# Sharing the state product between VectorE and GpSimd, and moving the cell gathers, in a one-core hybrid kernel

## The chip, the cores and the metric

The kernel runs on one core of a Trainium2 chip. The metric is device time of one execution, in microseconds, as the median of several runs. The core's engines are TensorE (PE; its weight loads are PEld), VectorE (DVE), ScalarE (ACT), GpSimd (POOL) and SyncE (SP), which here only issues transfers. L872 means line 872 of the kernel before.

## The reference, cut to what matters

A tensor x of 16 images x 32 channels x 16 x 16 pixels passes four layers, each added to the stream with a norm:

- L0: an attention over pixels with pooled keys.
- L1: a Mamba block. For 64 inner channels and 16 states it runs `h = exp(dt * A) * h + dt * u * B[t]` and `y = sum over n of h[n] * C[n]` over time, for every image.
- L2: a windowed attention with 8 heads, then a mixture of 8 experts, two of which are chosen for each token.
- L3: attention in blocks of 32 nodes. Its mask and weights come from 1,048,576 edges (row, column, value): an edge inside one block sets the mask of its cell to 1 and writes its value there; the last edge of a cell wins. Only rows and columns below 256 matter. Then a small feed-forward part whose steps are picked at run time.

The output is the stream after that, of the shape of x.

## The kernel before

Activations lie as 128 partitions (4 images x 32 channels) by 1,024 columns (4 groups of 256 pixels). Each engine has one instruction stream in a hand-written order; semaphores tie them together.

**Edges.** The edge list (8 MB) comes in four chunks of 2 MB (`load_edges`, L637) on SyncE's queue, between the small weight loads: chunk 0, W_p and w_o, chunk 1, the 37 loads of `load_w1`, chunks 2 and 3. ScalarE turns the integers of a chunk to floats (`edge_floats`, L952), GpSimd subtracts columns from scaled rows (`edge_keys`, L733), VectorE picks the 8 largest keys of every 256 (`edges`, L1215). Then VectorE sorts out 48 slots for each partition and computes their fields (L1334). For 16 slots at a time (`CHUNK`), `hot_rows` (L1360) makes one-hot rows on VectorE, `weigh_planes` (L618) makes weighed one-hot columns on GpSimd, and TensorE adds their products in PSUM (`put_chunk`, L1924). The planes that result are copied by ScalarE (L1076), turned by TensorE (L1938), and VectorE reads them off as a table that holds, for each of 8,192 cells, the number of its edge or none (`planes_to_table`, L1374; `table_indices`, L1368; semaphore `tab_dve`). GpSimd gathers the 64 columns of values with 64 indirect transfers of 128 elements (`gather`, L858), multiplies them with the mask (L931), stores both in DRAM (L935) and loads them in the form of the blocks (L940; semaphore `bias_in`). VectorE builds bias, mask and gates from them in `bias_and_gates` (L1572), called in the expert loop before its fifth step. If a partition had more edges than slots, a slow path would run; with this input it does not.

**The scan of L1.** 64 steps, i = 16 j + n, for the four groups j of 1,024 columns and the 16 states n (a partition holds a channel of one of two states' halves). For step i: SyncE loads B in broadcast form (two transfers of 256 KB, L673; four buffers, two of them in dA, which was also the buffer of one-hot rows); GpSimd multiplies it with dt * u to dBu (L872, two buffers), then issues gather i - 1; ScalarE computes exp(dt * A) into PSUM (L1090, two buffers); VectorE runs the recurrence of a whole step in one scan instruction (L1432, three buffers `h_buf`); TensorE spreads C over the partitions into banks 2 and 3 (L1997, one buffer); VectorE multiplies state and C to hC (L1450, two buffers); TensorE adds hC to the sum in banks 6 and 7 (L2013). VectorE's order is scan(i + 1), product(i). After the last product of a group VectorE gates it (`gate_group`, L1435). dt is a softplus; its last two steps (L854, L856) are done by VectorE for j = 0 and by GpSimd, before the scan, for j = 1 to 3.

**Behind the scan.** Output projection, norm, then GpSimd clears two buffers (L882 to L884), the window attention runs on all four compute engines (GpSimd in L908, L919, L921), then GpSimd goes on with the mask product and the bias transfers (L931 to L940), and with a buffer that keys need later (L947). The expert loop (L1624), norm(5) (L1638), and the block attention of L3 follow.

## Time and profile before

| | us |
|---|---|
| median of 3 runs | 687.41 (687.07 to 688.64) |
| profiled execution | 686.04 |
| its span | 684.4 |
| busy: TensorE | 442.3 (65%) |
| busy: VectorE | 492.1 (72%) |
| busy: ScalarE | 200.8 (29%) |
| busy: GpSimd | 347.5 (51%) |

The page gives busy times, the span in 40 slices, the chain of work that ended last, and the costliest groups of instructions. In the slices VectorE and GpSimd are both at nine tenths or more from the 9th or 10th slice to the 21st, which is the scan. In the chain, GpSimd has 28% of the span, VectorE 24%, TensorE 21% and issue 16%; the two largest lines are L872 (12%) and L859 (8%). TensorE's granted clock was 0.824 of 2.4 GHz on the mean. A line of the order of time holds start, duration, engine, line, operation, output and inputs with their shapes, the count, and in brackets how long the engine had idled and what released it; a merged line covers several instructions.

### The profile page before, as it was taken

Reading aid. Unit: us, or ns where it says so; the run is one execution under the profiler, and the core shown is the slowest. Engines: PE = TensorE matmul, PEld = TensorE weight load, DVE = VectorE, ACT = ScalarE, POOL = GpSimd, SP = SyncE. Lnnn points to the kernel's source line nnn. Section 1 sums busy time; section 2 is a strip of 40 time slices with the busy share of each in tenths; the row PEclk is TensorE's granted clock in tenths of the full one; section 3 lists DMA queues with packets and bytes.
Section 4 is the critical chain, followed back from the end, with each engine's and each line's share of the span. In section 5 each row is a group of like instructions: output and inputs, shape, how many; then the busy total and the mean of one; then the engine's idle time right before and its main releaser. Section 6 shows DMA issues by size and latency. Waiting matters only on the chain.

```text
span 684.4 us, 8165 instructions
## 1 busy us (share of the span) xinstructions
PE 442.3 (65%) x2986; PEld 225.9 (33%) x2986; DVE 492.1 (72%) x627; ACT 200.8 (29%) x218; POOL 347.5 (51%) x285
## 2 busy tenths in 40 slices
PE   7644864147767668667667887985579964525560
PEld 2531313113223223222223344654355633523220
DVE  2946995789999999999995348877135548996332
ACT  2463692033333332333330543121020043012110
POOL 6626307969999999999992003657840000000000
PEclk9866885559999999999999999555569997678766
DMA  8340020545555554454530000000000000000000
GB/s 281 63 196 0 10 66 13 123 120 143 154 147 148 154 151 151 145 151 144 150 93 1 11 1 1 2 1 2 9 13 0 1 0 1 1 1 0 8 5 31
DMA packets 29252, 46.04 MB, mean 67 GB/s; under 512 B 17878, under 2 KB 19320, under 8 KB 28184
## 3 DMA queue, kind: packets, MB, share of 16 engines
q1 hardware_dynamic: 26776, 45.10, 22.8%
q0 software_dynamic: 2368, 0.37, 0.4%
q8 instruction: 25, 0.41, 0.2%
q14 instruction: 19, 0.16, 0.1%
q10 hardware_dynamic: 64, 0.00, 0.0%
HBM read 43.55 MB, written 1.11 MB: 65 GB/s over the span
## 4 chain that ended last, share of the span: by engine, by line
POOL 28%; DVE 24%; PE 21%; issue 16%; SPq 4%; ACT 4%; DMA 2%; DVEq 0%; POOLq 0%; ACTq 0%
POOL dBu L872 12%; POOL hit L859 8%; SPq L651 3%; PE ps L1875 2%; PE ps L2184 2%; POOL work L921 2%; POOL work L919 2%; PE ps L2085 2%; POOL work L908 2%; PE ps L2195 2%; DMA work<-in_L_attn_edge_index 1%; POOL hst L621 1%; PE ps L2341 1%; PE ps L1929 1%; PE ps L2013 1%
## 5 line engine op out<-in xcount | busy, mean ns | idle before, releaser
L2013 PE MATMUL ps<-hC,ident 128*128 128x512 f32 x256 | 121.7, 597 | 0.0
L1090 ACT ACTIVATE ps<-work,a_neg 128x1020 f32<-128x1020 f32 x64 | 71.3, 1115 | 164.5 <-DVE hst L1432 99.1
L1432 DVE TENSOR_TENSOR_SCAN hst<-ps,dBu 128x1024 f32<-128x1024 f32 x43 | 98.2, 2285 | 3.9 <-issue 1.3
L1997 PE MATMUL ps<-late,pick_state 96*128 96x512 bf16 x128 | 39.5, 391 | 84.3 <-DVE hC L1450 65.2
L872 POOL TENSOR_TENSOR dBu<-work,dA 128x1024 f32<-128x1024 f32 x32 | 75.5, 2361 | 2.8 <-DVE hst L1432 2.2
L872 POOL TENSOR_TENSOR dBu<-work,b_sb 128x1024 f32<-128x1024 f32 x32 | 75.9, 2373 | 0.6
L859 POOL DMA_INDIRECT hit<-in_L_attn_edge_values,tab_i x64 | 63.4, 990 | 12.8 <-issue 10.0
L2013 PEld LDWEIGHTS ps<-hC,ident 128*128 128x128 f32 x256 | 49.3, 193 | 43.6 <-issue 34.6
L1997 PEld LDWEIGHTS ps<-late,pick_state 96*128 96x128 bf16 x128 | 7.8, 97 | 135.1 <-DVE hC L1450 112.6
L1450 DVE TENSOR_TENSOR hC<-hst,ps 128x1024 f32<-128x1024 f32 x43 | 51.4, 1195 | 1.2 <-PE ps L1997 1.2
L1432 DVE TENSOR_TENSOR_SCAN work<-ps,dBu 128x1024 f32<-128x1024 f32 x21 | 48.0, 2285 | 1.4
L1810 PE MATMUL ps<-idle_bf,zero_bf 128*128 128x512 bf16 x122 | 37.7, 450 | 16.8 <-issue 13.4
L908 POOL TENSOR_TENSOR work<-work,sm 128x1024 f32<-128x1024 f32 x8 | 15.3, 1911 | 55.0 <-DVE sm L1537 55.0
L1000 ACT ACTIVATE sq<-ps 128x512 f32<-128x512 f32 x12 | 7.2, 597 | 85.7 <-PE ps L1875 68.4
L1522 DVE COPY_PREDICATED work<-band,ps 128x1024 f32<-128x1024 int32 x8 | 10.4, 1305 | 24.4 <-ACT work L1115 24.4
L621 POOL TENSOR_TENSOR hst<-hC,b_sb 128x2048 bf16<-128x2048 bf16 x3 | 11.8, 3934 | 30.6 <-DVE dBu L1364 27.1
L1450 DVE TENSOR_TENSOR hC<-work,ps 128x1024 f32<-128x1024 f32 x21 | 25.1, 1195 | 1.5 <-PE ps L1997 1.5
L1810 PEld LDWEIGHTS ps<-idle_bf,zero_bf 128*128 128x128 bf16 x122 | 12.1, 109 | 40.7 <-issue 29.7
L2138 PE MATMUL ps<-work 128*32 128x64 f32 (+1 forms) x512 | 14.6, 306 | 14.1 <-POOL work L921 14.1
L2114 PEld LDWEIGHTS ps<-work 32*128 32x128 f32 x512 | 21.5, 256 | 5.0 <-issue 5.0
L2114 PE MATMUL ps<-work 32*128 32x64 f32 x512 | 22.8, 346 | 0.0
L2126 PE MATMUL ps<-work,w_vu 32*128 32x256 f32 x64 | 15.9, 584 | 8.4 <-DVE work L1551 8.4
(358 smaller groups left out, 857.9 us busy)
## 6 DMA issues: line engine op xcount, KB each, us to landing
b_sb<-b_rows_all SPq DMA_DIRECT2D x64, 256.0 KB
dA<-b_rows_all SPq DMA_DIRECT2D x64, 256.0 KB
work<-in_L_attn_edge_index SPq DMA_DIRECT2D x6, 1024.0 KB, 6.3
dA<-in_L_attn_edge_index SPq DMA_DIRECT2D x1, 1024.0 KB, 10.5
dBu<-in_L_attn_edge_index SPq DMA_DIRECT2D x1, 1024.0 KB, 12.5
hit<-in_L_attn_edge_values,tab_i POOLq DMA_INDIRECT x64
late<-work SPq DMA_DIRECT2D x12, 64.0 KB, 2.0
X<-in_x SPq DMA_DIRECT2D x1, 512.0 KB, 3.9
```

Of the source, the lines that this page charges most:

```text
L621: return eng.tensor_tensor(plane_hot[k], col_hot[:, r, :].unsqueeze(2).to_broadcast([P, CHUNK, PLANES, C]), weighed[:, r, :].unsqueeze(3). ...
L651: sp.dma_start(dst, src).then_inc(dma_w1, 16)
L859: nc.gpsimd.indirect_dma_start(out=hit[:, i // C, 0, i % C:i % C + 1], out_offset=None, in_=a["L3_attn_edge_values"].rearrange("(e o) -> e ...
L872: nc.gpsimd.tensor_tensor(dBu[:, i % 2, :], dtu[:, j * NT:(j + 1) * NT], b_buf[i % 4], ALU.mult).then_inc(dbu_done, 1)
L908: nc.gpsimd.tensor_tensor(pairs(s2_buf[u % 3]), pairs(s2_buf[u % 3]), sm2[:, u % 2, :].unsqueeze(2).to_broadcast([P, SEGS, C]), ALU.mult). ...
L1090: nc.scalar.activation(dst[:, :, 1:], src[:, :, 1:], ACT.Exp, scale=a_neg[:, n:n + 1]).then_inc(dA_sb, 1)
L1432: V.tensor_tensor_scan(h_buf[i % 3], dA_ps[k], dBu[:, k, :], 0.0, ALU.mult, ALU.add).then_inc(scan_done, 1)
L1450: V.tensor_tensor(hC[:, k, :], h_buf[i % 3], bank(2, 2), ALU.mult).then_inc(hc_done, 1)
L1810: T.matmul(bank(k), zero_bf[:, :], idle_bf[:, :], start=True, stop=True, skip_group_check=True)
L1997: last = T.matmul(bank(2 + h), pick_state[:, n, :, :].rearrange("p v i -> p (v i)"), parts[:, j * NT + h * HALF:j * NT + (h + 1) * HALF], ...
L2013: last = T.matmul(bank(6 + h), ident[:, :], hC[:, i % 2, h * HALF:(h + 1) * HALF], start=False, stop=(n == S - 1))
L2114: last = T.matmul(bank(g)[:, 2 * C * m:2 * C * m + 2 * C], qm[r, j * WT + m, 4 * hg:4 * hg + 4, :].rearrange("p h q -> p (h q)"), xpad[r, ...
```

## The change

- The product of state and C (hC) is split by columns: VectorE takes the first 848 of 1,024 (704 in the last group), GpSimd the others. GpSimd can't read PSUM, so ScalarE copies these columns of the spread C into `c_sb` first; VectorE, too, waits for that copy. TensorE's second half of the sum waits for GpSimd's part.
- No gathers in the scan. 5 stand behind the table, 15 behind the clearing of the expert buffers, 44 behind the window attention. GpSimd's order in the scan is dBu(i + 2), share(i).
- GpSimd's part of dt for groups 1 to 3 moves into the scan, in pieces of 256 columns, one in every third state up to the tenth of the group before.
- `weigh_planes` is done by VectorE, in front of each block of one-hot rows; TensorE waits for one semaphore less.
- The planes are turned as before; ScalarE copies the turned planes to SBUF, the scan starts after that, and VectorE reads the table from the copy behind the last scan product, ahead of the last gating.
- `bias_and_gates` moves from the expert loop to the place between the expert output and norm(5).
- SyncE: the loads of L1 are fewer (24 for 37, some of them over more partitions with a repeated source); chunk 2 of the edges is issued after the 11th; the loads of B for step 0 are issued at once, for step 1 after the third block of one-hot rows, from step 2 on after the planes.
- ScalarE converts chunk 2 behind the copies of the turned attention and chunk 3 behind the first norm's root. GpSimd's key subtraction of chunk 2 moves ahead of the weight taps. TensorE's idle matmuls after L0 are 18 for 10.

```diff
@@ -139,6 +139,9 @@
         b_rows = area(0, 1)
+        DVE_COLS = (848, 848, 848, 704)
+        c_sb = [area(4, 1)[:, k * 320:(k + 1) * 320] for k in range(3)]
+        EARLY = 20
         b_dram = nc.dram_tensor("b_rows_all", [J, 2 * S, NT], F32, kind="Internal").ap()
@@ -235,9 +238,9 @@
         planes = area(22, 1).rearrange("p (g r) -> p g r", g=G)
...
-        inv_i = hC[:, 1, 0:G * 2 * C].rearrange("p (g c) -> p g c", g=G).bitcast(I32)
-        symbols = hC[:, 1, G * 2 * C:G * 2 * C * PLANES].rearrange("p (g k c) -> p g k c", g=G, c=2 * C)
+        turned = area(0, 1).rearrange("p (g r) -> p g r", g=G)
+        table_at = area(1, 1)
@@ -499,12 +504,13 @@
         def load_w1():
+            over = lambda n, v: bass.AP(v.tensor, v.offset, [[0, n]] + [list(x) for x in v.ap])
+            split = lambda n, t: t
             col = lambda v: v.rearrange("(c o) -> c o", o=1)
+            for dst, name in ((ln_g, "gamma"), (ln_b, "beta"), (b_p[:, :], "b_p")):
+                yield split(G, dst), over(G, col(a["L1_conv_" + name]))
             for g in range(G):
                 r = slice(C * g, C * g + C)
-                yield ln_g[r], col(a["L1_conv_gamma"])
-                yield ln_b[r], col(a["L1_conv_beta"])
-                yield b_p[r, :], col(a["L1_conv_b_p"])
                 yield win_nat[r, :, :], a["L1_conv_W_in"].rearrange("(r e) c -> e r c", e=C)
@@ -512,12 +518,11 @@
             yield s2[:, :], broadcast_rows(a["L1_conv_s2"], P)
+            for dst, name in ((conv_b, "conv_b"), (b_dt, "b_dt"), (d_skip, "D_skip")):
+                yield split(2, dst[:, :]), over(2, col(a["L1_conv_" + name]))
+            yield split(2, a_log[:, :]), over(2, a["L1_conv_A_log"])
             for v in range(2):
                 r = slice(64 * v, 64 * v + 64)
-                yield conv_b[r, :], col(a["L1_conv_conv_b"])
-                yield b_dt[r, :], col(a["L1_conv_b_dt"])
-                yield d_skip[r, :], col(a["L1_conv_D_skip"])
-                yield a_log[r, :], a["L1_conv_A_log"]
                 yield wx_t[r, :], a["L1_conv_W_x"].rearrange("n d -> d n")
@@ -647,9 +652,10 @@
             with nc.allow_non_contiguous_dma("small transposed weights"):
-                for dst, src in load_w1():
+                for k, (dst, src) in enumerate(load_w1()):
                     sp.dma_start(dst, src).then_inc(dma_w1, 16)
-            load_edges(2)
+                    if k == 10:
+                        load_edges(2)
             load_edges(3)
@@ -663,10 +669,13 @@
             sp.wait_ge(b_out, 16)
-            sp.wait_ge(planes_ps, 1)
             late_weights = load_w3()
...
                 j, n = i // S, i % S
+                if i == 1:
+                    sp.wait_ge(rows_sb, 3)
+                if i == 2:
+                    sp.wait_ge(planes_ps, 1)
                 if i >= 4:
@@ -801,6 +810,7 @@
                                   .to_broadcast([BC, S, 2, 64])).then_inc(w_rows_sb, 1)
+            edge_keys(2)
             pool.wait_ge(w1_dve, 1)
@@ -842,19 +851,6 @@
-            for q in range(SLOTS // CHUNK):
-                pool.wait_ge(rows_sb, max(2, q + 1))
-                if q >= 2:
-                    pool.wait_ge(hot_used, q - 1)
-                weigh_planes(nc.gpsimd, q % 2, q).then_inc(hot_sb, 1)
...
-            for j in range(1, J):
-                r = slice(j * NT, (j + 1) * NT)
-                pool.wait_ge(dt_log, j + 1)
-                nc.gpsimd.tensor_tensor(dt_act[:, r], dt_act[:, r], dtu[:, r], ALU.add).then_inc(dt_later, 1)
-                pool.wait_ge(dt_later, j)
-                link(nc.gpsimd.tensor_tensor(dtu[:, r], dt_act[:, r], u_act[:, r], ALU.mult))
...
             def gather(i, done=gathered):
@@ -862,32 +858,61 @@
-            for i in range(J * S):
+            def state_input(i):
...
                 j, n = i // S, i % S
...
                     pool.wait_ge(dtu_sb, 1)
+                    pool.wait_ge(hot_used, 2)
                 pool.wait_ge(b_in[i % 4], 32 * (i // 4 + 1))
...
                                         ALU.mult).then_inc(dbu_done, 1)
-                if i == 1:
-                    pool.wait_ge(tab_dve, 1)
-                if i >= 1:
-                    gather(i - 1)
-            gather(J * S - 1)
...
+            def state_share(i):
...
+                pool.wait_ge(scan_done, i + 1)
+                pool.wait_ge(c_copied, i + 1)
+                if i >= 2:
+                    pool.wait_ge(y_ps, i - 1)
+                cols = DVE_COLS[i // S]
+                nc.gpsimd.tensor_tensor(hC[:, i % 2, cols:], h_buf[i % 3][:, cols:], c_sb[i % 3][:, 0:NT - cols],
+                                        ALU.mult).then_inc(hc_pool, 1)
...
+            def later_delta(j, quarter):
...
+                r = slice(j * NT + quarter * N, j * NT + (quarter + 1) * N)
+                pool.wait_ge(dt_log, j + 1)
+                nc.gpsimd.tensor_tensor(dt_act[:, r], dt_act[:, r], dtu[:, r], ALU.add).then_inc(dt_later, 1)
+                pool.wait_ge(dt_later, 4 * (j - 1) + quarter + 1)
+                link(nc.gpsimd.tensor_tensor(dtu[:, r], dt_act[:, r], u_act[:, r], ALU.mult))
...
+            state_input(0)
+            state_input(1)
+            for i in range(J * S):
+                if i + 2 < J * S:
+                    state_input(i + 2)
+                state_share(i)
+                j, n = i // S, i % S
+                if j + 1 < J and n % 3 == 0 and n < 12:
+                    later_delta(j + 1, n // 3)
             assert J * S == 2 * C
...
+            pool.wait_ge(tab_dve, 1)
+            nc.gpsimd.memset(xpad[:, :, 0:C], 0.0).then_inc(filled, 1)
+            for i in range(EARLY // 4):
+                gather(i)
             pool.wait_ge(x_new, 2 * 2)
-            nc.gpsimd.memset(xpad[:, :, 0:C], 0.0).then_inc(filled, 1)
             nc.gpsimd.memset(eb_bd, 0.0)
             nc.gpsimd.memset(e_bd, 0.0).then_inc(filled, 1)
+            for i in range(EARLY // 4, EARLY):
+                gather(i)
...
             with pool.If(more > 0):
-                pool.wait_ge(gathered, 16 * 2 * C)
+                pool.wait_ge(gathered, 16 * EARLY)
                 with pool.Fori(0, EDGES // (P * GW)) as t:
@@ -927,6 +952,8 @@
             window_bands(UNITS - 1)
+            for i in range(EARLY, 2 * C):
+                gather(i)
             pool.wait_ge(gathered, 16 * 2 * C)
@@ -976,11 +1003,10 @@
                 nc.scalar.activation(pixels(att, h), pixels(att, h), ACT.Exp).then_inc(first_sb, 1)
-            edge_floats(2)
             for h in range(2):
...
                 nc.scalar.activation(pixels(att_t, h), bank(2 * h, 2), ACT.Copy).then_inc(first_sb, 1)
-            edge_floats(3)
+            edge_floats(2)
@@ -1006,6 +1032,7 @@
             inverse_root(rs4[:, :], bn2[:, :, 1], eps5).then_inc(rs4_sb, 1)
+            edge_floats(3)
@@ -1074,6 +1101,19 @@
             nc.scalar.activation(planes, ps[:, 0:4, 0:N], ACT.Copy).then_inc(planes_sb, 1)
+            act.wait_ge(b_out, 16)
+            act.wait_ge(planes_t, 1)
+            act.wait_ge(over_sb, 1)
+            nc.scalar.activation(turned, ps[:, 0:4, 0:N], ACT.Copy).then_inc(turned_sb, 1)
...
+            def state_out(i):
...
+                act.wait_ge(c_ps, i + 1)
+                if i >= 3:
+                    act.wait_ge(hc_pool, i - 2)
+                cols = DVE_COLS[i // S]
+                nc.scalar.activation(c_sb[i % 3][:, 0:NT - cols], bank(2, 2)[:, cols:],
+                                     ACT.Copy).then_inc(c_copied, 1)
@@ -1084,11 +1124,14 @@
                 elif n == 0:
-                    act.wait_ge(dt_later, j)
+                    act.wait_ge(dt_later, 4 * j)
                 src = dt_act[:, j * NT:(j + 1) * NT].rearrange("p (b t) -> p b t", t=N)
...
                                      scale=a_neg[:, n:n + 1]).then_inc(dA_sb, 1)
+                if i >= 1:
+                    state_out(i - 1)
+            state_out(J * S - 1)
             norm_steps(2, eps5)
@@ -1371,10 +1414,12 @@
-            def planes_to_table(dst, base, link):
...
-                weights = ps[:, 0:4, 0:2 * C]
-                shares = ps[:, 0:4, 2 * C:2 * C * PLANES].rearrange("p g (k c) -> p g k c", c=2 * C)
+            def planes_to_table(dst, base, link, source, room):
...
+                weights = source[:, :, 0:2 * C]
+                shares = source[:, :, 2 * C:2 * C * PLANES].rearrange("p g (k c) -> p g k c", c=2 * C)
+                inv_i = room[:, 0:G * 2 * C].rearrange("p (g c) -> p g c", g=G).bitcast(I32)
+                symbols = room[:, G * 2 * C:G * 2 * C * PLANES].rearrange("p (g k c) -> p g k c", g=G, c=2 * C)
                 k3_ = PLANES - 1
@@ -1403,11 +1448,11 @@
             dve.wait_ge(cols_sb, 1)
-            for q in range(2):
-                hot_rows(q, q).then_inc(rows_sb, 1)
...
-            dve.wait_ge(hot_used, 1)
-            hot_rows(0, 2).then_inc(rows_sb, 1)
+            for q in range(SLOTS // CHUNK):
+                if q >= 2:
+                    dve.wait_ge(hot_used, q - 1)
+                weigh_planes(V, q % 2, q)
+                hot_rows(q % 2, q).then_inc(rows_sb, 1)
             dve.wait_ge(dt_log, 1)
@@ -1415,11 +1460,9 @@
             V.tensor_copy(over_i[:, :], bank(0)[0:1, HALF - 1:HALF]).then_inc(over_sb, 1)
-            link(planes_to_table(tab[:, :], g_base[:, 0, :], link))
-            table_indices(link).then_inc(tab_dve, 1)
...
             dve.wait_ge(part_round, PARTS)
             dve.wait_ge(b_rows_sb, 1)
+            dve.wait_ge(turned_sb, 1)
             V.memset(dA_ps[0][:, 0:NT:N], 0.0)
@@ -1429,6 +1472,7 @@
                     dve.wait_ge(hc_done, i - 2)
+                    dve.wait_ge(hc_pool, i - 2)
                 V.tensor_tensor_scan(h_buf[i % 3], dA_ps[k], dBu[:, k, :], 0.0, ALU.mult,
@@ -1444,12 +1488,17 @@
                 dve.wait_ge(scan_done, i + 1)
-                dve.wait_ge(c_ps, i + 1)
+                dve.wait_ge(c_copied, i + 1)
                 if i >= 2:
                     dve.wait_ge(y_ps, i - 1)
-                V.tensor_tensor(hC[:, k, :], h_buf[i % 3], bank(2, 2), ALU.mult).then_inc(hc_done, 1)
+                cols = DVE_COLS[j]
+                V.tensor_tensor(hC[:, k, 0:cols], h_buf[i % 3][:, 0:cols], bank(2, 2)[:, 0:cols],
+                                ALU.mult).then_inc(hc_done, 1)
                 if n == 0 and j > 0:
                     gate_group(j - 1)
+            dve.wait_ge(turned_sb, 1)
+            link(planes_to_table(tab[:, :], g_base[:, 0, :], link, turned, table_at))
+            table_indices(link).then_inc(tab_dve, 1)
             gate_group(J - 1)
@@ -1622,8 +1671,6 @@
             for t in range(TT):
-                if t == 4:
-                    bias_and_gates()
                 dve.wait_ge(ex_ps, t + 1)
@@ -1635,6 +1682,7 @@
+            bias_and_gates()
             norm(5)
@@ -1868,7 +1916,7 @@
                     last.then_inc(first_ps, 1)
-            keep_warm(10, 7)
+            keep_warm(18, 7)
@@ -1978,7 +2026,6 @@
                 pe.wait_ge(rows_sb, q + 1)
-                pe.wait_ge(hot_sb, q + 1)
                 ends = q == SLOTS // CHUNK - 1
@@ -1992,7 +2039,7 @@
                     pe.wait_ge(c_in, 16 * PARTS * J)
-                    pe.wait_ge(tab_dve, 1)
+                    pe.wait_ge(turned_sb, 1)
                 for h in range(2):
@@ -2010,6 +2057,8 @@
                 for h in range(2):
+                    if h == 1:
+                        pe.wait_ge(hc_pool, i + 1)
                     last = T.matmul(bank(6 + h), ident[:, :], hC[:, i % 2, h * HALF:(h + 1) * HALF],
```

## Rows read from the trace of the kernel before

**Rows 1.** Order of time in the scan, GpSimd and VectorE: start, us, engine, line.

```profile
247.18 2.36 POOL L872 TENSOR_TENSOR dBu<-work,dA 128x1024 f32<-128x1024 f32 x1
...
249.57 2.29 DVE L1432 TENSOR_TENSOR_SCAN hst<-ps,dBu 128x1024 f32<-128x1024 f32 x1
```

**Rows 2.** Order of time, GpSimd at the end of the scan.

```profile
362.62 0.99 POOL L859 DMA_INDIRECT hit<-in_L_attn_edge_values,tab_i  x1 [0.16 <-issue]
363.91 0.94 POOL L859 DMA_INDIRECT hit<-in_L_attn_edge_values,tab_i  x1 [0.30 <-issue]
```

**Rows 3.** Order of time, two of VectorE's products early in the scan.

```profile
158.47 1.20 DVE L1450 TENSOR_TENSOR hC<-hst,ps 128x1024 f32<-128x1024 f32 x1
...
161.78 1.19 DVE L1450 TENSOR_TENSOR hC<-hst,ps 128x1024 f32<-128x1024 f32 x1
```

**Rows 4.** Order of time from 30 to 68 us.

```profile
30.32 0.85 SPq L640 DMA_DIRECT2D work<-in_L_attn_edge_index  x2
...
39.25 1.91 ACT L955 ACTIVATE work<-work 128x2048 f32<-128x2048 int32 x1 [10.57 <-DMA work<-in_L_attn_edge_index]
...
47.67 0.75 DVE L1274 SCALAR_TENSOR_TENSOR X<-ps,gamma,X 128x512 f32<-128x512 f32 x1 [8.45 <-PE ps L1865]
...
62.93 1.41 DVE L1222 MAX8 hC<-work 128x8 f32<-128x256 f32 x4 [3.24 <-POOL work L738]
...
66.67 1.87 DVE L1310 TENSOR_SCALAR x<-xn,w_in 128x512 f32<-128x512 f32 x1
```

**Rows 5.** Order of time from 94 to 145 us.

```profile
94.73 1.76 DVE L1356 TENSOR_TENSOR hC<-rows_at,b_sb 128x1536 bf16<-128x1536 bf16 x1
...
96.52 3.23 DVE L1364 TENSOR_SCALAR dA<-rows_at,b_sb 128x256 bf16<-128x256 bf16 x16
...
118.38 3.60 PE L1929 MATMUL ps<-dA,hst 32*128 32x256 bf16 x64 [5.28 <-POOL hst L621]
...
124.31 0.40 DVE L1379 TENSOR_SCALAR hC<-ps 128x256 int32<-128x256 int32 x1
...
142.49 4.47 DVE L1432 TENSOR_TENSOR_SCAN hst<-ps,dBu 128x1024 f32<-128x1024 f32 x2 [1.25 <-issue]
```

**Rows 6.** Order of time in the scan: TensorE's broadcast of C, ScalarE's exponential.

```profile
249.50 0.60 PE L1997 MATMUL ps<-late,pick_state 96*128 96x512 bf16 x2 [1.20 <-DVE hC L1450]
...
251.90 1.12 ACT L1090 ACTIVATE ps<-work,a_neg 128x1020 f32<-128x1020 f32 x1 [2.41 <-DVE hst L1432]
```

**Rows 7.** Groups of GpSimd's instructions by line and form: count, busy us, mean ns.

```profile
L921 POOL TENSOR_TENSOR work<-work,band 128x896 f32<-128x896 f32 x8 | 16.6, 2076 | 0.0
...
L806 POOL TENSOR_TENSOR work<-w_in,work 128x256 f32<-128x256 f32 x2 | 1.7, 851 | 18.4 <-DVE w_dt L1305 18.4
...
L769 POOL TENSOR_TENSOR centerer<-ident,averager 128x128 f32<-128x128 f32 x1 | 0.5, 455 | 0.1
```

**Rows 8.** Order of time, VectorE's last gating behind the scan.

```profile
373.46 1.22 DVE L1438 TENSOR_TENSOR work<-work,ps 128x1024 f32<-128x1024 f32 x1 [5.59 <-PE ps L2013]
```

**Rows 9.** Order of time from 489 to 557 us: GpSimd, then VectorE, then TensorE.

```profile
489.96 0.31 POOL L931 TENSOR_TENSOR hit<-hit 128x64 f32<-128x64 f32 x1
...
493.73 4.64 POOL L940 DMA_DIRECT2D late<-cell_bias  x8 [1.59 <-DMA cell_bias<-hit]
...
529.12 0.07 DVE L1576 MEMSET late<- 128x8 f32 x1
...
536.16 1.22 DVE L1631 TENSOR_TENSOR work<-ps,work 128x1024 f32<-128x1024 f32 x1 [0.44 <-PE ps L2195]
...
554.40 0.69 DVE L1293 TENSOR_TENSOR xn<-ps,rstd 128x512 f32<-128x512 f32 x1 [3.93 <-ACT rstd L995]
...
556.39 3.70 PE L1815 MATMUL ps<-xn,nat 128*128 128x512 f32 x8 [1.25 <-DVE xn L1293]
```

**Rows 10.** Order of time, GpSimd's first instruction of the window attention.

```profile
414.72 1.91 POOL L908 TENSOR_TENSOR work<-work,sm 128x1024 f32<-128x1024 f32 x1 [29.81 <-DVE sm L1537]
```

**Rows 11.** Busy times in stretches: length, each engine's busy us, granted clock, DMA.

```profile
565.00:570.00 5.00, 2.64 (x11) 1.17 (x12) 4.51 (x5) 2.03 (x2) 0.00 (x0) 0.61 0.00 0
```

9 lines of the change are left out of this document (5 added, 4 removed).

## The prediction

> **What bounds the kernel now.** I read the page first (busy shares, the 40 slices, the chain that ended last), then the order of time in four stretches: 30 to 70 us, 92 to 145 us, some steps of the scan, and 486 to 570 us. The scan is a third of the span and VectorE is nearly always busy there, yet it isn't the bound. GpSimd multiplies dBu in 2.36 us [rows 1], idles 0.16 us, issues a gather in 0.99 us [rows 2] and goes straight on to the next product: 3.53 us, all of it GpSimd's own work. VectorE's scan (249.57) starts just as that product ends (247.18 + 2.36 = 249.54). Where GpSimd is not late, VectorE's products follow each other after 3.31 us [rows 3]. So the scan runs at GpSimd's pace, and the chain of waits passes through dBu and the gathers, hardly through the product hC.
>
> **Part 1, the first 80 us.** [rows 4] ScalarE waits 10.57 us for chunk 2 of the edges, converts it, and only then copies the turned attention, for which TensorE and then VectorE (8.45 us of idle time) wait. The chunk was issued at 30.32, after 37 small loads, and landed by 39.25. In the change it is issued after 11 of 24 loads (about 15 us) and converted behind the copies, so its landing, 8.9 us after issue by this row and some more behind chunk 1, no longer decides; VectorE is free at 47.67 - 8.45 = 39.2, and the attention's output can be there by then. Chunk 3 is converted behind the first norm's root, near 43 us; issued near 25 us it has landed. GpSimd subtracts the keys 13 to 18 us earlier, so VectorE's wait for them (3.24) goes, and with it the lengthening of the affine step beside one: 1.87 us for 512 columns, where a product of 1,024 columns takes 1.19 [rows 3], so about 0.6 would do, 1.3 less. Sum: 8.45 + 3.24 + 1.3 = 13.0 us. From there VectorE has an unbroken queue to the slot columns, so all of it arrives. Bounds: 8.5 (keys still late, or the 8 added warm-up matmuls outlast the weights at the low clock) to 14.
>
> **Part 2, the planes.** [rows 5] From the first block of compares (96.52) to the first scan (142.49) it is 46.0 us: weighing on GpSimd, a third block behind it, the table read while GpSimd multiplies. Now VectorE weighs before each block. That isn't in the trace; a product of 1,536 bf16 columns took 1.76, so 2,048 take 2.3, and a block of compares 3.2: 3 x 5.5 = 16.5. Then TensorE's last chunk 3.6; planes copied, turned and the overflow flag read, 2.3 (from 121.98 to 124.31); ScalarE's new copy of the turned planes 1.0 (estimate: 1,024 columns, as the exponential's 1.12 [rows 6]); hand-overs 0.5; and 1.3 from the cleared columns to the first scan, as now (141.23 to 142.49). That is 25.2, a gain of 20.8 us. Bounds 17 (weighing at twice the row) to 22. SyncE's loads of B for states 1 and 2 wait for block 3 and the planes, with the rest of B queued behind; the first state's no longer does. A product dBu after them has about 2 us to spare before its scan, so this hides.
>
> **Part 3, the scan.** The gather leaves GpSimd's step; a share of hC comes in, 176 of 1,024 columns, 320 in the last quarter. The same operation takes 0.455 us at 128 columns and 2.076 at 896, which gives 0.55 and 0.86, less 0.03 of overlap; the 256-column row of 0.851 (other strides) is the upper end [rows 7]. I take the line, since the share is contiguous as its two ends are. GpSimd's step: 2.32 + 0.52 = 2.84, in the last quarter 3.15. In the first three quarters GpSimd also computes the next delta in four pieces of two 256-column products, 2 x 0.72 + 0.15 = 1.6 each. A quarter is 16 x 2.84 + 6.4 = 51.8, three times, then 50.4: 205.8. VectorE alone: 3.31 less 0.18 (0.33 in the last quarter), 3.13 and 2.98, with three gatings 201. GpSimd stays the bound, by little. Before, it is 225.4 from the first scan's start to the last product's end (367.87, 5.59 before the gating of [rows 8]). With 1 us for start and end the gain is 18.5 us; bounds 4 (share and pieces at 0.851) to 24 (VectorE's pace). The new waits: GpSimd's share waits for ScalarE's copy, and behind it in GpSimd's queue stands the product dBu of three states on. The copy comes after the product (0.93), TensorE's broadcast (0.60) and itself, 0.3 to 0.5: 2.0 us after a scan's end, while dBu ends at 2.3 [rows 6]. Hidden, with 0.3 us to spare. TensorE's second half of the sum waits for the share, which precedes VectorE's part: hidden.
>
> **Part 4, the table behind the scan.** 13 operations of the bias step, most on 256 columns, take 5.4 us (529.12 to 536.16 - 0.44 - 1.22) [rows 9]; the table's 15 have about 1,000 columns more: 6.2. They lie in the 5.59 us in which VectorE waits for TensorE before the last gating [rows 8]. Cost 0.6; with that cover gone, 6.2. Five gathers then run beside the norm, where VectorE has two SBUF-to-SBUF affine steps; no gather stands beside one in the trace. Between 0 and 2 x 0.99 [rows 2]: 0.5.
> The Trainium skill (SBUF — State Buffer, Who interferes with whom) says that GpSimd and a VectorE operation in a two-port mode, or one with two SBUF inputs against a GpSimd read, block each other for a whole instruction. The trace agrees for products (the 1.87 above); for gathers no run here shows it. By it this term would be up to 2.0.
>
> **Part 5, the late gathers.** All 64 lay under the scan's pace; now 5 come behind it, 15 behind its output (20 us in 29.8 us of idle time [rows 10]) and 44 after the window attention. Two gathers without a product between them start 1.29 us apart [rows 2]. From 490.0: 44 x 1.29 = 56.8, the last one out by 546.6, landed by 548.3 (1.6, as the 1.59 that GpSimd waited for its own store). From the mask product (489.96) to the bias in SBUF: issues to 498.37 and a landing of 1.6, 10.0 us [rows 9]. The bias lands at 558.2. VectorE, free at 550.5, builds it until 563.6 and norms in 1.3: 564.9 against 556.3, 8.6 us lost. In the experts' loop the removed step gives nothing: the next product but one waited for TensorE anyway (0.44). TensorE now idles 10 us before eight matmuls that took 3.70; after the next idle stretch, of 6 us, its granted clock was 0.61 [rows 11], halfway down to 1.2 GHz, and at that level they take 7.4: I add 3.0. Sum 11.6 lost.
> The Trainium skill (DMA: Bandwidth & Descriptors, Latency and other measured facts) gives about 1 us for GpSimd's emission of a software DMA. The trace agrees with the busy part (0.99) and shows 0.30 us of idle time on top. By the page alone, an estimate, 44 take 44 us and this is rival (a).
>
> **Sum.** -13.0 - 20.8 - 18.5 + 0.6 + 0.5 + 11.6 = -39.6 us. The profiled execution took 686.04 us (span 684.4), 1.4 below the median of the runs: 646.4, and 647.8 as a median. Measurement here tells 0.2% (1.4 us) from no change.
>
> **Rivals.** (a) The gathers go out at their busy time, 1.0 us: the bias lands at 546, in time; the moved step then costs what it exceeds VectorE's wait for the root (5.4 against 3.93 [rows 9]), 1.5, and no clock is lost: 637.7. Against it stands the one pair. It decides at 1.1 us apart. (b) The share and the pieces are dear, 0.85: the scan gains 4 only, 662. (c) On SyncE's one queue the small loads stand behind the 2 MB of chunk 2 and hold the first norms; part 1 gives 5: 656. Against: 13 loads are out 15 us before they are read. (d) Gathers hold up the router's 17 short VectorE operations, most with two SBUF inputs, each by up to one gather of 0.99, some 10 us in all: 658; this is the skill's lock, told above, with the trace silent. (e) Slower: ScalarE's copy stands behind an exponential, 1.12 us [rows 6]. It is ready 3.1 us after a scan's end, GpSimd waits 0.8 in each step, and a step costs 3.65, with the delta pieces 4.05: the scan takes 33 us more than before, against 21.1 gained elsewhere: 699. It decides from 3.88 us a step. Against: in ScalarE's order the copy of state i precedes the exponential of i + 2. (f) The edits do not take effect on the path at all: 687; each moves work off a stretch that waits, so 1 in 100.
>
> **Chances.** Forecast 0.52 (its own bounds 640 to 655), (a) 0.17, (b) 0.12, (c) 0.08, (d) 0.07, (e) 0.03, (f) 0.01. The range takes in (a), (c), (d) and most of (b): 635 to 660. Faster 0.96, same 0.01, slower 0.03.
>
> **What the profile after would show.** Part 1: the attention's residual on VectorE near 39 us. Part 2: the first scan near 108. Part 3: dBu products 2.84 apart where no delta piece stands between, 3.15 at the end, GpSimd hardly idle; if it waits for the scan instead, VectorE is the bound. Part 4: the last gating at most 1 us behind TensorE. Part 5: 1.29 between gathers, VectorE waiting for the bias, a lower clock in the four projections. Wrong altogether if a scan step exceeds 3.5 us.

## The result, and the profile after

The changed kernel takes 701.25 us (median of 4 runs, 701.0 to 702.52) where before takes 687.89 (4 runs, 687.07 to 688.64): the ratio is 1.0199, with a 95% interval of 1.0183 to 1.0215. So it takes 2.0% longer, clear of no change, though the interval reaches to both sides of 2%; and it is 53 us above the forecast. The span of the profiled execution is 699.5 us. Of all runs named here one, of the kernel before beside the fifth experiment (1,408.53 us), was a slow one and is left out.

The page of after, busy times and slices (each slice is 17.5 us):

```profile
PE 449.7 (64%) x2994; PEld 229.3 (33%) x2994; DVE 470.2 (67%) x630; ACT 217.6 (31%) x283; POOL 369.9 (53%) x364
DVE  3989987999999999996126878200052468976421
POOL 6574017999999999993531765977760000000000
PEclk9888877999999999999979555556559986768775
```

The scan ends in slice 19 (317 us), three slices earlier than before. But slices 27 to 29 are nearly empty for DVE (0 0 0, from 455 to 507 us), exactly where GpSimd shows 7, 7 and 7: the late gathers. To see where that gap begins, both orders of time are cut at the same operations:

| stretch | before | after | difference |
|---|---|---|---|
| start to the first scan | 142.49 | 108.10 | -34.4 |
| scans, to the last product's end | 225.4 | 209.0 | -16.4 |
| table, gating, projection, norm | 11.3 | 12.5 | +1.3 |
| norm to the window attention's input | 8.4 | 11.2 | +2.8 |
| from there to the first unit's weights on GpSimd | 27.2 | 36.1 | +8.9 |
| window units, to the last band product | 75.3 | 75.2 | 0 |
| to VectorE's residual X | 1.9 | 13.5 | +11.6 |
| to the copy of the router's results | 16.9 | 48.5 | +31.7 |
| experts, to their residual | 40.4 | 41.5 | +1.1 |
| to norm(5), with the moved bias step in after | 5.2 | 6.6 | +1.4 |
| block attention, to its residual | 68.3 | 69.4 | +1.1 |
| to the first pick of the last part | 8.7 | 8.7 | 0 |
| the steps picked at run time, to the end | 53.0 | 59.1 | +6.0 |

Up to the norm behind the scan the change gained 49.5 us, nearly the 51.2 that the forecast had to there. Then 55.0 us are lost in four stretches, in each of which, or just ahead of it, gathers go out back to back, and 6.0 in the last steps. These are the rows of after that answer to those shown of before. VectorE, in order of time, for [rows 4, 5]:

```profile
39.12 0.73 DVE L1317 SCALAR_TENSOR_TENSOR X<-ps,gamma,X 128x512 f32<-128x512 f32 x1
...
94.36 2.28 DVE L626 TENSOR_TENSOR hst<-hC,b_sb 128x2048 bf16<-128x2048 bf16 x1
96.56 3.22 DVE L1407 TENSOR_SCALAR dA<-rows_at,b_sb 128x256 bf16<-128x256 bf16 x16
...
105.29 0.15 DVE L1462 CAST over_i<-ps 1x1 int32<-1x1 f32 x1 [3.12 <-PE ps L1986]
...
108.10 2.29 DVE L1476 TENSOR_TENSOR_SCAN hst<-ps,dBu 128x1024 f32<-128x1024 f32 x1 [1.25 <-ACT ps L1130]
```

One step of the scan, for [rows 1, 3, 6, 7]:

```profile
252.69 0.55 POOL L880 TENSOR_TENSOR hC<-hst,work 128x176 f32<-128x176 f32 x1
252.77 2.29 DVE L1476 TENSOR_TENSOR_SCAN work<-ps,dBu 128x1024 f32<-128x1024 f32 x1 [0.60 <-POOL dBu L870]
252.86 0.32 ACT L1115 ACTIVATE work<-ps 128x176 f32<-128x176 f32 x1 [1.81 <-PE ps L2044]
253.07 1.11 ACT L1130 ACTIVATE ps<-work,a_neg 128x1020 f32<-128x1020 f32 x1
253.21 2.35 POOL L870 TENSOR_TENSOR dBu<-work,b_sb 128x1024 f32<-128x1024 f32 x1
254.97 1.01 DVE L1495 TENSOR_TENSOR hC<-hst,ps 128x848 f32<-128x848 f32 x1
```

The share takes 0.55 us as forecast, and ScalarE's copy stands ahead of the exponential and costs 0.32.

Now the stretch behind the window attention. VectorE and TensorE, for [rows 9]:

```profile
465.73 1.41 DVE L1616 SCALAR_TENSOR_TENSOR X<-ps,b_u,X 128x512 f32<-128x512 f32 x2 [20.91 <-remote]
...
514.26 0.42 DVE L1651 COPY work<-ps 128x256 f32<-128x256 f32 x1 [35.24 <-remote]
```

```profile
454.29 0.42 PE L2187 MATMUL ps<-work 128*32 128x64 f32 x6 [0.28 <-issue]
455.02 0.35 PE L2187 MATMUL ps<-work 128*32 128x32 f32 x5 [0.30 <-issue]
466.53 3.78 PE L1923 MATMUL ps<-X,centerer 128*128 128x512 f32 x4 [11.17 <-issue]
...
488.14 0.21 PE L2222 MATMUL ps<-rb_row,one_row 1*128 1x32 f32 x1 [0.82 <-issue]
490.24 0.21 PE L2223 MATMUL ps<-r_bd,xn 128*128 128x32 f32 x1 [1.90 <-issue]
493.04 0.21 PE L2223 MATMUL ps<-r_bd,xn 128*128 128x32 f32 x1 [2.59 <-issue]
```

In before the same two instructions of VectorE, residual and copy, stand 16.9 us apart, and their waits are put down to TensorE:

```profile
491.95 1.41 DVE L1567 SCALAR_TENSOR_TENSOR X<-ps,b_u,X 128x512 f32<-128x512 f32 x2 [9.35 <-PE ps L2138]
...
508.81 0.42 DVE L1602 COPY work<-ps 128x256 f32<-128x256 f32 x1 [7.15 <-PE ps L2174]
```

In after, too, both of VectorE's waits are for TensorE: for the last window output, and for the last of 32 router matmuls. TensorE stands idle between matmuls that wait for no semaphore ("issue"), and its records lie a multiple of 0.70 us apart (488.14, 488.84 for a weight load, 490.24, 491.64, 493.04). The trace notes the semaphore of the last matmul (record 493.04) only at 514.24; so a record here does not tell when the work was done, and what is held up must be read from VectorE's side. The 128x512 matmuls of the norm take 3.78 us as in before: long ones are not slower. In the trace of before no matmul without a wait of its own is held like that.

Meanwhile GpSimd keeps its pace, as forecast from [rows 2]:

```profile
452.36 0.99 POOL L855 DMA_INDIRECT hit<-in_L_attn_edge_values,tab_i  x1 [0.15 <-issue]
453.65 0.94 POOL L855 DMA_INDIRECT hit<-in_L_attn_edge_values,tab_i  x1 [0.30 <-issue]
...
509.06 0.32 POOL L958 TENSOR_TENSOR hit<-hit 128x64 f32<-128x64 f32 x1 [2.02 <-DMA hit<-in_L_attn_edge_values,tab_i]
...
512.83 4.65 POOL L967 DMA_DIRECT2D late<-cell_bias  x8 [1.59 <-DMA cell_bias<-hit]
```

The bias lands near 519, 67 us behind the last band product (68.2 in the forecast). It is wanted at 557. The wait that the forecast had priced never happened, because all else was later.

### The profile page after: what moved, and what is told of

Read it like the earlier page. It is cut to its first block, busy times and chain, and to the rows that moved or that the text cites. A ratio compares the mean times of both kernels' runs of the same rounds, so it can differ in the third digit from the quotient of the medians.

```text
span 699.5 us, 8496 instructions
## 1 busy us (share of the span) xinstructions
PE 449.7 (64%) x2994; PEld 229.3 (33%) x2994; DVE 470.2 (67%) x630; ACT 217.6 (31%) x283; POOL 369.9 (53%) x364
## 4 chain that ended last, share of the span: by engine, by line
DVE 34%; PE 25%; issue 15%; ACT 10%; POOL 8%; another core or an unknown queue 5%; DVEq 1%; DMA 1%; ACTq 0%; POOLq 0%
DVE hC L1495 8%; ACT ps L1130 7%; PE ps L2044 5%; PE ps L2244 2%; PE ps L2134 2%; PE ps L2233 2%; POOL work L946 2%; PE ps L1923 2%; POOL dBu L870 2%; DVE hC L1269 2%; POOL work L944 2%; POOL work L933 2%; PE ps L1863 2%; DVE hC L1265 2%
## 5 line engine op out<-in xcount | busy, mean ns | idle before, releaser
L870 POOL TENSOR_TENSOR dBu<-work,b_sb 128x1024 f32<-128x1024 f32 x32 | 75.3, 2353 | 41.4 <-DVE work L1459 39.2
L855 POOL DMA_INDIRECT hit<-in_L_attn_edge_values,tab_i x64 | 60.8, 950 | 19.1 <-issue 19.1
L1115 ACT ACTIVATE work<-ps 128x176 f32<-128x176 f32 (+1 forms) x64 | 22.2, 347 | 121.4 <-PE ps L2044 121.4
L1858 PE MATMUL ps<-idle_bf,zero_bf 128*128 128x512 bf16 x130 | 40.0, 451 | 16.8 <-issue 14.6
L1495 DVE TENSOR_TENSOR hC<-hst,ps 128x848 f32<-128x848 f32 (+1 forms) x43 | 41.8, 973 | 1.2 <-ACT work L1115 1.2
L2244 PE MATMUL ps<-x,xn 128*128 128x512 f32 x32 | 18.0, 698 | 24.2 <-DVE work L1662 24.2
L880 POOL TENSOR_TENSOR hC<-hst,work 128x176 f32<-128x176 f32 (+1 forms) x43 | 27.4, 636 | 2.3 <-ACT work L1115 2.3
L2163 PE MATMUL ps<-work 32*128 32x64 f32 x512 | 25.6, 353 | 4.5 <-issue 4.5
L2163 PEld LDWEIGHTS ps<-work 32*128 32x128 f32 x512 | 23.5, 262 | 10.2 <-issue 10.2
```

The source lines that it names most:

```text
L855: nc.gpsimd.indirect_dma_start(out=hit[:, i // C, 0, i % C:i % C + 1], out_offset=None, in_=a["L3_attn_edge_values"].rearrange("(e o) -> e ...
L870: nc.gpsimd.tensor_tensor(dBu[:, i % 2, :], dtu[:, j * NT:(j + 1) * NT], b_buf[i % 4], ALU.mult).then_inc(dbu_done, 1)
L880: nc.gpsimd.tensor_tensor(hC[:, i % 2, cols:], h_buf[i % 3][:, cols:], c_sb[i % 3][:, 0:NT - cols], ALU.mult).then_inc(hc_pool, 1)
L1495: V.tensor_tensor(hC[:, k, 0:cols], h_buf[i % 3][:, 0:cols], bank(2, 2)[:, 0:cols], ALU.mult).then_inc(hc_done, 1)
L1858: T.matmul(bank(k), zero_bf[:, :], idle_bf[:, :], start=True, stop=True, skip_group_check=True)
L2163: last = T.matmul(bank(g)[:, 2 * C * m:2 * C * m + 2 * C], qm[r, j * WT + m, 4 * hg:4 * hg + 4, :].rearrange("p h q -> p (h q)"), xpad[r, ...
```

## The experiments

**Theory G:** gathers that go out back to back hold up the issue of instructions on TensorE, and so each stretch in which it issues many short ones. In the scan of before, where nothing of the kind is seen, they went out 3.53 us apart:

```profile
246.17 0.99 POOL L859 DMA_INDIRECT hit<-in_L_attn_edge_values,tab_i  x1 [0.16 <-issue]
...
249.70 0.99 POOL L859 DMA_INDIRECT hit<-in_L_attn_edge_values,tab_i  x1 [0.16 <-issue]
```

**Rivals:** B, any unbroken run of GpSimd does it; C, it is the moved bias step and TensorE's low clock, not the gathers; a price for each gather, wherever it stands; and S, the many reads of one address. For the last 6 us, **theory L:** the place of the loop's code in the instruction stream.

### The late gathers left out, replaced, drawn apart, made direct

The first and the fourth edit are shown against the kernel after, the second and the third against the first. The values that these kernels leave out or get wrong are read only behind the copy of the router's results.

```diff
-            for i in range(EARLY, 2 * C):
-                gather(i)
-            pool.wait_ge(gathered, 16 * 2 * C)
+            nc.gpsimd.memset(hit[:, 0, 0, EARLY:C], 0.0)
+            link(nc.gpsimd.memset(hit[:, 1, 0, :], 0.0))
+            pool.wait_ge(gathered, 16 * EARLY)
```

> The kernel after without its 44 late gathers (two memsets write their cells instead, so values are left out). Theory G (gathers that go out back to back hold up TensorE where it runs many small matmuls): the window attention still starts 11.7 us late behind the 15 gathers ahead of it, but from its last GpSimd product (452) the residual follows after 2 us, and the router's copy 17 us after the residual as before, not 48.5: COPY near 471, and 175.6 us from there to the end as before plus 1.5 for the moved bias step: 649 us. Rival C (TensorE's low clock or the moved bias step itself is what costs): the router's stretch stays near 48 us and the time near 695.

In the second kernel a memset stands for each gather:

```diff
+            for i in range(EARLY, 2 * C):
+                link(nc.gpsimd.memset(dBu[:, 0, :], 0.0))
```

> The kernel after with each of the 44 late gathers replaced by a GpSimd memset of 1,024 columns (0.94 us, as a gather's busy time; values left out). Theory G: the stall belongs to the gathers as transfers: no stall, 650 us. Rival B (any unbroken run of GpSimd instructions holds TensorE up): residual to router copy stays near 48 us, time near 700.

In the third, 14 gathers with fillers:

```diff
+            for i in range(EARLY, EARLY + 14):
+                gather(i)
+                link(nc.gpsimd.memset(dBu[:, :, :], 0.0))
+                link(nc.gpsimd.memset(dBu[:, 0, 0:512], 0.0))
```

> The kernel after with 14 of the 44 late gathers, each followed by two memsets so that they go out about 3.5 us apart as in the scan of before (30 left out). If the stall needs gathers close together (theory G with density): no instruction of TensorE stalls, residual to router copy 17 us, time 651. If each gather has its price whatever the distance (43 us / 44 = 1.0 each): 14 us more, 665.

In the fourth, all 44 as plain transfers:

```diff
-                gather(i)
+                nc.gpsimd.dma_start(hit[:, i // C, 0, i % C:i % C + 1],
+                                    a["L3_attn_edge_values"][P * i:P * i + P].rearrange("(p o) -> p o", o=1)
+                                    ).then_inc(gathered, 16)
```

> The kernel after with the 44 late gathers as plain GpSimd transfers of 128 x 4 bytes from the values (wrong values, indices left out). If software transfers of many small pieces are the cause, whatever computes their addresses: the same stall, time 690 to 705. If it is the gather's indirect form: no stall, 650 or less.

Measured, one run each, beside one of before of 689.75 us: 659.52, 659.61, 661.45 and 658.10 us. The kernel with 14 gathers 3.63 us apart, VectorE:

```profile
455.67 1.41 DVE L1620 SCALAR_TENSOR_TENSOR X<-ps,b_u,X 128x512 f32<-128x512 f32 x2 [9.65 <-PE ps L2191]
...
472.33 0.43 DVE L1655 COPY work<-ps 128x256 f32<-128x256 f32 x1 [7.81 <-PE ps L2227]
```

From residual to copy it is 16.7 us in all four (before 16.9, after 48.5), and VectorE's releaser is TensorE again. B falls: 44 memsets hold nothing up. C falls: the copy comes at 470.7 without late gathers, as expected near 471. A fixed price falls, at least at 3.63 us apart. And it is the gather's form, or something that comes with it, since plain transfers of 128 x 4 bytes went out 0.54 us apart (13 in 7.03 us), more than twice as densely, and held nothing up:

```profile
453.32 7.03 POOL L956 DMA_DIRECT2D hit<-in_L_attn_edge_values  x13
```

Nor is it the traffic that the transfers make. The software queue carried as many packets in the kernel after as in the one with plain transfers:

```profile
q0 software_dynamic: 2368, 0.37, 0.4%
```

```profile
q0 software_dynamic: 2368, 0.37, 0.5%
```

The times were 8 to 11 us above what was expected (649 to 651). I had carried the end of before over unchanged; in the first of these kernels the last steps take 60.5 us for 53.0, and the block attention 2.3 us more. So the last steps are a loss of their own.

### All gathers kept, but apart; the distance; the addresses

The fifth kernel puts a memset behind each gather outside the window attention, puts 24 gathers inside it, and the bias step behind norm(5):

```diff
+            def spaced(i):
+                gather(i)
+                link(nc.gpsimd.memset(dBu[:, 0, :], 0.0))
...
                 if u >= 1:
                     window_bands(u - 1)
+                for i in range(EARLY + 3 * u, EARLY + 3 * u + 3):
+                    gather(i)
```

> The kernel after with all 64 gathers kept but drawn apart: 20 ahead of the window attention and 20 behind it each followed by a memset (about 2.3 us apart), 24 inside it (three in a row behind each unit's band products); the bias step behind norm(5), in VectorE's 5.5 us wait for the projections. If gathers 2.3 us apart and three in a row hold nothing up: the 2.8 + 8.9 + 11.6 + 31.7 = 55 us of held-up stretches and 1.4 us of the bias step go: 701.25 - 56.4 = 645 us. If every gather has its price whatever the distance: 64 x 1.0 stay, 695 to 705. If three in a row already stall: 650 to 670.

The sixth, against the first:

```diff
+            for i in range(EARLY, EARLY + 22):
+                gather(i)
+                link(nc.gpsimd.memset(dBu[:, 0, :], 0.0))
```

> The kernel after with 22 of the 44 late gathers, one memset behind each, so about 2.3 us apart (22 left out). At 3.63 us apart nothing stalled (661.45 us, router's copy 16.7 us behind the residual). If the limit lies below 2.3 us: again 661. If the stall grows steadily with density: router's copy 25 us or more behind the residual, 670 to 680.

The seventh, against after:

```diff
-                    in_offset=bass.IndirectOffsetOnAxis(ap=tab_i[:, i:i + 1], axis=0)).then_inc(done, 16)
+                    in_offset=bass.IndirectOffsetOnAxis(ap=any_i[:, i:i + 1], axis=0)).then_inc(done, 16)
...
+            link(nc.gpsimd.iota(any_i[:, :], pattern=[[1, 2 * C]], base=0, channel_multiplier=8192))
```

> The kernel after with every gather reading 128 different addresses, spread over the whole list (values not the table's). In the table only 2,417 of 8,192 cells hold an edge, the others all read edge 0. Rival S (it is the many reads of one address, which the direct transfers did not have either): no stall, 650 to 660 us. If it is the gather's form and pace: unchanged, 48.5 us from residual to router copy, 701.

Spread, the kernel takes 661.33 us (two runs) against 687.57 and 689.69 for before, a ratio of 0.9603 (0.9518 to 0.9689): 40 us better than after, 4% better than before. Residual and copy stand where they should (2.1 us and 16.7), but 645 was missed by 16. GpSimd came to the first unit's weights at 372.33, 3.9 us after VectorE had its sums ready; the units took 83.4 us for 75.3, since three gathers with their gaps filled up to 4.5 us of a unit (384.21 to 388.69), more than the 4.2 us that GpSimd idles there in before, and GpSimd then worked without a break; the last steps took 59.6 us. The total lies in the range that was expected if three in a row already stall (650 to 670), and only the trace speaks for the other reading. The sixth kernel (one run), at 2.19 us apart, had 16.7 us from residual to copy, and took 662.25: no stall there. In the seventh (one run) all 64 gathers read different addresses, and it took 47.2 us from residual to copy (468.21 to 515.45), with the same records 1.40 us apart at the end of the router. S falls. Its total, 901.6 us, says nothing on this: with other values in the mask one of the last steps alone took 197 us, which I did not follow up.

### The code's place, first try

```diff
+            for _ in range(PAD):
+                dve.wait_ge(x_new, 1)
```

> The kernel after with 63 added wait instructions on VectorE, all already met, in its 19 us wait ahead of the first window unit; nothing else changed. VectorE's stream in after is 65 instructions longer than before ahead of the final steps, and in those steps it stands still 3.1 us behind two branches beside 8 KB instruction loads, which before does not show. Theory L (the code's place decides whether the loop's branches wait for code): 65 + 63 = 128 instructions of 64 bytes are one load, the steps return to their 53.0 us from the first pick to the end (59.1 in after): 695 us. If it is something else: 701.

It measured 717.72 us (one run), 16.5 more than after, and not what either theory expects; all of it lies between the norm behind the scan and the first unit's weights (63.7 us for 47.3). The kernel sets the name PAD itself further down, so 144 wait instructions came in, not 63, and the question of theory L was not put. But the run shows what the stall is better than any other. All 144 waits were already met; this is VectorE's own queue at that line, with least, median and longest duration in ns and first and last start:

```profile
L1565 DVEq EVENT_SEMAPHORE  x144: 1/50/709, 337.1 to 365.2; - x144
```

At its ordinary pace VectorE gets through such waits every 0.098 us, all 144 in 14 us; here they take 28. The 15 gathers ahead of the window attention go out from 337.7 to 356.1. From 340.9 to 359.0, about 3 us behind both, a record of these trivial waits lasts 0.70 us time and again, with a few short ones between (a selection, start and duration in us):

```text
340.824 0.050 Vector EVENT_SEMAPHORE
340.922 0.269 Vector EVENT_SEMAPHORE
342.649 0.706 Vector EVENT_SEMAPHORE
343.374 0.696 Vector EVENT_SEMAPHORE
...
357.544 0.695 Vector EVENT_SEMAPHORE
359.093 0.050 Vector EVENT_SEMAPHORE
359.191 0.050 Vector EVENT_SEMAPHORE
```

These instructions touch no SBUF and no PSUM, and VectorE is another engine than TensorE. So the instructions themselves are held back, on both engines, in pieces of 0.70 us: I call it their issue, though the records do not tell whether they are late in being issued or late in reaching the engine.

### Gathers placed by what TensorE issues, and the code's place again

Against the fifth kernel, with 18 gathers inside the window attention and 21 ahead of it:

```diff
-            for i in range(EARLY // 4, EARLY):
-                spaced(i)
+            for i in range(5, 15):
+                gather(i)
+            for i in range(15, EARLY):
+                spaced(i)
...
+                if u < INSIDE // 3:
+                    for i in range(EARLY + 3 * u, EARLY + 3 * u + 3):
+                        gather(i)
```

> As e5_spread, but the gathers placed by what TensorE issues: 5 drawn apart behind the scan, 10 back to back while TensorE runs only 512-column matmuls, 6 drawn apart ahead of the window units, three in a row behind each of the first six units and none behind the last two, 25 drawn apart behind the window attention. In e5_spread GpSimd came to the first unit's weights 3.9 us late and the units took 83.4 us for 75.3: 3.9 and some 6 of the 8.1 should go: 651 us. If the ten back to back hold TensorE up all the same: 660.

The tenth adds 63 instructions to VectorE, counted this time:

```diff
+            for k in range(FILL):
+                V.memset(pad[:, k:k + 1], 0.0)
             dve.wait_ge(o2_ps, UNITS)
```

> As e9_placed with 63 one-element memsets more on VectorE, in its 9.4 us wait for the window output (e8_pad had meant to add 63 and added 144). 65 + 63 = 128 instructions of 64 bytes make one 8 KB load, so the final loop stands to the loads as in before. Theory L (position of the loop's code): from the first pick to the end 53 us for 59, 6 us less than e9_placed: 645 us. If it is something else: no difference.

Measured: 655.68 us (ratio to before 0.954, 0.9524 to 0.9556) and 649.85 us (0.9453, 0.9437 to 0.9468), each 5 us above what was expected (651 and 645). In the ninth kernel the ten gathers back to back do hold TensorE up: VectorE's first masking of scores (356.25) comes 18.2 us behind the window attention's input, for 14.3 in before, while GpSimd stands idle for 8.9 us until it gets the first unit's weights. And the units took 78.9 us for 75.3.

The 63 useless instructions make the kernel 5.8 us faster. One of the last steps, VectorE, in the ninth and then the tenth kernel:

```profile
613.49 0.14 DVE L1772 CAST ctrl<-code 1x1 int32<-1x1 f32 x1
...
628.01 2.47 DVE L1837 TENSOR_SCALAR work<-ps,work 128x1024 f32<-128x1024 f32 x2 [11.73 <-PE ps L2391]
...
636.65 0.14 DVE L1772 CAST ctrl<-code 1x1 int32<-1x1 f32 x1
```

```profile
615.29 0.14 DVE L1776 CAST ctrl<-code 1x1 int32<-1x1 f32 x1
...
625.13 2.47 DVE L1841 TENSOR_SCALAR work<-ps,work 128x1024 f32<-128x1024 f32 x2 [7.04 <-PE ps L2395]
...
634.65 0.14 DVE L1776 CAST ctrl<-code 1x1 int32<-1x1 f32 x1
```

23.2 us from the second pick to the third fall to 19.4, and 39.6 from the second pick to the end to 33.2. The loads of 8 KB of instructions from the first pick to the end, in the queue table of that stretch, for the ninth and then the tenth:

```profile
q14 instruction: 11, 0.09, 0.5%
```

```profile
q14 instruction: 3, 0.02, 0.1%
```

Before has 4 of them, after 11. Theory L holds, and the other kernels bear it out. With 754, 755 or 881 instructions on VectorE ahead of the first pick (before, the eleventh, the tenth and the twelfth) there are 3 or 4 such loads, and 52.0 to 53.8 us to the end; with 818, 819 or 963 there are 11 loads and 58.8 to 61.6 us in all nine that make three picks. That 128 instructions make one load is an estimate from the 16 KB loads of after: 25 of them for the 5,988 matmuls and weight loads of TensorE, 68 bytes each. The Trainium skill (Runtime: NRT & Kernel Launch, Instruction fetch mechanics) says that a taken branch to code outside the two loaded pages has to wait for it; the trace agrees, with 3.1 us from VectorE's branch at 663.57 in after to its next instruction at 666.73. It gives pages of 16 KiB; the loads here are of 8 KB.

### In the kernel before, the gathers moved, and the bias step

```diff
-                if i >= 1:
-                    gather(i - 1)
-            gather(J * S - 1)
...
+            for i in range(20, 2 * C):
+                gather(i)
             pool.wait_ge(gathered, 16 * 2 * C)
...
-                if t == 4:
-                    bias_and_gates()
...
+            bias_and_gates()
             norm(5)
```

> The kernel before with nothing changed but the place of the gathers (5, 15 and 44, as in after) and of the bias step. Theory G: its scan falls to VectorE's pace (3.31 for 3.53: 13.5 us less), the held-up stretches are those of after (2.8 + 8.9 + 11.6 + 31.7 = 55 us more), with 3 for the bias step and the clock: 687.9 - 13.5 + 58 = 732 us. If the stall needed anything else of the change: 680 or less.

It measured 733.77 us (two runs), a ratio of 1.0672 (1.065 to 1.0693). The scans take 6.8 us less, not 13.5 (from the first scan to the last one's start 213.2 us for 220.0), the stretch from residual to copy 45.2 us (510.17 to 555.35), the one to the residual 17.3. So the stall needs none of the other edits of the change; the bias step stands behind all of these stretches. And the last steps take 52.0 us here: the stall alone does not lengthen them.

### Closer again

The last edit is shown against the tenth kernel. Beside it fewer gathers stand where they had cost: 3 behind the scan, 8 back to back and 6 drawn apart ahead of the window units, 13 inside them, 34 behind.

```diff
             for i in range(EARLY + INSIDE, 2 * C):
-                spaced(i)
+                gather(i)
+                link(nc.gpsimd.memset(dBu[:, 0, 0:256], 0.0))
```

> As e10_placed_pad with fewer gathers where they cost (3 behind the scan, 8 back to back, 6 drawn apart, 3 + 5 x 2 inside the window attention) and 34 behind it, each followed by a memset of 256 columns only: about 1.5 us apart, between 1.25 (stalls) and 2.19 (none). If 1.5 us is far enough: router's copy 17 us behind the residual, 643 to 646 us. If the issue of all engines is held at this distance too: copy 25 us or more behind the residual, 655 to 670 us.

It measured 641.56 us (641.29 to 643.9, 4 runs; expected 643 to 646), a ratio to before of 0.9333 (0.9318 to 0.9349): the best kernel of this study, 60 us faster than after. GpSimd and VectorE:

```profile
443.19 0.99 POOL L858 DMA_INDIRECT hit<-in_L_attn_edge_values,tab_i  x1 [0.16 <-issue]
444.17 0.33 POOL L971 MEMSET dBu<- 128x256 f32 x1
444.77 0.95 POOL L858 DMA_INDIRECT hit<-in_L_attn_edge_values,tab_i  x1 [0.27 <-POOL dBu L971]
...
446.23 1.41 DVE L1633 SCALAR_TENSOR_TENSOR X<-ps,b_u,X 128x512 f32<-128x512 f32 x2 [9.49 <-PE ps L2204]
...
463.20 0.42 DVE L1668 COPY work<-ps 128x256 f32<-128x256 f32 x1 [6.97 <-PE ps L2240]
```

At 1.55 us apart the residual comes 3.2 us behind the last band product (2.1 at 2.19), and the copy 17.0 behind it. A distance 0.3 us larger than that of after turns 43.3 us of stall into about 1. With 34 gathers for 44 it is not their number. The window units, with two gathers in most, take 75.0 us, and the first masking comes 14.8 us behind the input: eight back to back, beside 512-column matmuls, cost 0.5 us where ten had cost 3.9.

## Why the prediction was wrong, point by point

**Part 1, -13.0:** right. The residual is at 39.12 (near 39 was forecast), and VectorE begins the planes at 83.68 for 96.52: 12.8.

**Part 2, -20.8:** right. From the planes' start to the first scan it is 24.4 us (25.2), a gain of 21.6. Weighing takes 2.29 (2.3), the first scan starts at 108.10 (near 108).

**Part 3, -18.5:** right in mechanism, 2 us too good. dBu products stand 2.83 apart early in the scan (151.16 to 153.99), GpSimd's share takes 0.55 and 0.86, and the scans 209.0 us for the forecast 206.8. The bound shifts between the engines, which the sum by quarters had left out: in steps without a delta piece VectorE's 3.13 is the longer, in those with one GpSimd's, and the slack of the one doesn't make up for the other. Rivals (b), (c) and (e) did not come, nor (a): the pace of 1.25 us is above the 1.1 from which it decides. That the measured 701 lies near the 699 of (e) is chance: no step of the scan waits as (e) has it.

**Part 4, +1.1:** right: +1.3 from the last product to the norm.

**Part 5, +11.6:** wrong, and this is the step that failed: it put what the gathers take from other engines at nothing. All that lies behind the norm that follows the scan costs 64.6 us: 55.0 in the four held-up stretches, 3.6 in the experts, the moved bias step and the block attention, and 6.0 in the last steps. The arithmetic of part 5 held: 1.25 us apart (1.29), the bias 67 us behind the window attention (68.2). What failed is the question asked. I priced the 64 gathers by GpSimd's time and by who waits for the bias, and looked at neighbours only where SBUF is shared, at VectorE. Nowhere did I ask what transfers issued in so dense a run take from the issue of other engines. The evidence that they take nothing came from the scan, where they stand 3.53 us apart, and that is no evidence for 1.25; the one pair 1.29 us apart [rows 2] was read for its pace alone. Of the four stretches lost, two (2.8 and 8.9 us) lie beside the 20 gathers that I had put in idle time of GpSimd, at 0.5 in all. The cause of the first, 2.8 us, stays in part open: with these gathers 2.2 us apart it took 10.9, 10.8 and 10.5 us (fifth, ninth and twelfth kernel) for 11.2, and 8.4 before. There TensorE halts twice among 128 matmuls of 32 columns, beside a 16 KB load of its own code (at 330.2 in after), which in before had come 2.7 us ahead of them; and in the eleventh kernel such a halt, 1.43 us at 373.06, comes with a load at 371.9 and no gather since 359.5. So what is shown to be the gathers' is 52.2 us, in the other three. The clock's share was small: 1.1 us in the experts and 1.7 in VectorE's wait for the projections (5.49 for 3.79, at a granted clock of 0.72 from 563 to 569 us, where before has 1.00), for the 3.0 given.

**Rival (d)** had the right place for a wrong reason: the router's VectorE operations keep their 0.42 us and run when the gathers are out. (The 1.87 us that part 4 reads as beside a product stood beside a subtraction and a memset of GpSimd.) The lock of the Trainium skill (SBUF — State Buffer, Who interferes with whom) is there in both directions, with other neighbours and for a microsecond at a time. In the fifth kernel a gather that begins beside VectorE's subtraction of two SBUF inputs (383.20) lasts 1.79 us for 0.95, and the affine step beside GpSimd's memsets and gathers 1.56 for 0.55:

```profile
331.47 1.56 DVE L1515 TENSOR_SCALAR xn<-xn,w_in 128x512 f32<-128x512 f32 x1
...
383.20 2.10 DVE L1586 TENSOR_TENSOR work<-work,mx 128x1024 f32<-128x1024 f32 x1
384.38 1.79 POOL L855 DMA_INDIRECT hit<-in_L_attn_edge_values,tab_i  x1 [0.16 <-issue]
```

**The last steps, +6.0:** not in the forecast at all. The change adds 65 instructions to VectorE ahead of the loop, most of them waits that got an instruction of their own, and so moves the loop's code against the loads.

**The range** of 635 to 660 and the 0.96 for faster were too sure: apart from (d), with 10 us on VectorE, no case stood for the moved work's effect on engines that it doesn't feed. With the gathers placed as in the twelfth kernel and the loop's code in place, the idea of the change gives 641.56 us, inside that range.

**What stays open:** why an indirect gather holds the instructions of other engines and a plain transfer doesn't; what the 0.70 us are; whether the instructions are late in being issued or in reaching the engine; whether three gathers in a row inside a window unit hold anything up; and whether ScalarE and SyncE are held too, as they issued too little there to show it.
